# GpSimd in place of VectorE for the low part of the gate weights in a mixture-of-experts kernel

## The reference

```python
weights, idx = top 2 of 8 experts for each token, from softmax(x @ gate_w.T)
h1 = einsum('td,efd->etf', x, w1) + b1        # gate weights w1, w3: 512 x 256 for each expert
h3 = einsum('td,efd->etf', x, w3) + b3
a  = swiglu(h1 * h3)                          # g = min(h[::2], 7), l = clip(h[1::2], -7, 7)
                                              # g * sigmoid(1.702 g) * (l + 1)
y  = einsum('etf,edf->etd', a, w2) + b2
out = sum over the two experts of weight * y + shared expert(x)
```

## Time and profile before

| | |
|---|---|
| median of 3 runs | 2312.86 us (2309.55 to 2316.68) |
| the profiled execution | 2297.38 us, of which the span is 2295.6 us |
| mean granted TensorE clock | 0.96 of 2.4 GHz |
| busy over the span | PE 90%, DVE 66%, ACT 74%, POOL 28% |
| L2057, the subtraction that the change moves | 43 instructions of 2.29 us |
| L1776, the additions | 142 instructions, 2.05 us each on average |

### The profile page before, as it was taken

One profiled execution on the slowest core, in us unless ns is written; L12 is line 12 of the kernel. 1 busy time (PEld: TensorE's weight loads), 2 busy tenths in 40 slices (PEclk: granted clock), 3 DMA queues, 4 the chain that ended last, 5 costly groups with the idle time before them and its releaser, 6 DMA issues. The chain is left out here.

```text
span 2295.6 us, 38125 instructions
## 1 busy us (share of the span) xinstructions
PE 2074.2 (90%) x14085; PEld 1267.4 (55%) x14085; DVE 1521.9 (66%) x2352; ACT 1701.4 (74%) x2162; POOL 645.4 (28%) x639
## 2 busy tenths in 40 slices
PE   5995999999999999999998794799999999999970
PEld 4783333333333333333332784688888888888860
DVE  4664255555555555555555896677789988998875
ACT  4663999999999999999997672433466666666645
POOL 1111000000000000000000451677345565555637
PEclk9997999999999999999999996899999999999995
DMA  5886655555444456555410682455567676677756
GB/s 184 307 290 194 139 104 105 105 102 90 73 87 87 90 100 105 105 102 75 58 37 21 220 272 108 164 179 173 193 194 208 179 179 176 173 182 178 175 167 254
DMA packets 162651, 340.50 MB, mean 148 GB/s; under 512 B 17768, under 2 KB 91624, under 8 KB 155176
## 3 DMA queue, kind: packets, MB, share of 16 engines
q1 hardware_dynamic: 130220, 284.42, 46.5%
q0 software_dynamic: 29936, 45.90, 10.7%
q10 hardware_dynamic: 2316, 7.80, 1.0%
HBM read 194.29 MB, written 143.62 MB: 147 GB/s over the span
## 5 line engine op out<-in xcount | busy, mean ns | idle before, releaser
L1108 ACT ACTIVATE att_prob<-att_scores 128x1024 f32<-128x1024 f32 (+2 forms) x1122 | 997.7, 1031 | 58.5 <-PE att_scores L1054 54.9
L1073 PE MATMUL att_out<-att_prob,att_va 128*32 128x512 f32 (+3 forms) x5000 | 576.5, 541 | 12.9 <-DVE att_prob L1140 12.9
L1054 PE MATMUL att_scores<-att_qs,att_ks 50*128 50x512 f32 (+3 forms) x2560 | 465.5, 430 | 21.2 <-DMA att_qs<-guard 17.1
L1054 PEld LDWEIGHTS att_scores<-att_qs,att_ks 50*128 50x128 f32 x2560 | 210.9, 185 | 492.5 <-ACT att_prob L1108 417.9
L1776 POOL DMA_INDIRECT sums<-moe_y,moe_token x142 | 290.9, 2048 | 265.5 <-ACT moe_y L2034 225.2
L1918 PE MATMUL moe_ps<-moe_xt_hi,moe_w_hi 128*128 128x512 f32 (+1 forms) x880 | 339.8, 386 | 10.1 <-ACT moe_h L2007 7.1
L1918 PE MATMUL moe_ps<-moe_xt_hi,moe_w_lo 128*128 128x512 f32 (+1 forms) x880 | 333.4, 379 | 0.0
L1918 PE MATMUL moe_ps<-moe_xt_lo,moe_w_hi 128*128 128x512 f32 (+1 forms) x880 | 331.9, 377 | 0.0
L1002 POOL DMA_DIRECT2D ctx_scr<-att_cout x64 | 55.1, 860 | 983.0 <-DVE att_cout L1190 944.1
L1140 DVE SCALAR_TENSOR_TENSOR att_prob<-att_prob,att_tri 128x512 f32<-128x512 f32 x224 | 144.8, 688 | 269.0 <-ACT att_prob L1108 269.0
L1073 PEld LDWEIGHTS att_out<-att_prob,att_va 128*32 128x32 f32 x5000 | 108.3, 108 | 186.3 <-issue 105.5
(11 more groups left out here) (259 smaller groups left out, 3257.5 us busy)
## 6 DMA issues: line engine op xcount, KB each, us to landing
qk_parts<-proj_qk SPq DMA_DIRECT2D x64, 512.0 KB, 4.2
keep_first_weights<-w_experts SPq DMA_DIRECT2D x22, 1412.0 KB, 6.6
moe_wraw<-w_experts SPq DMA_DIRECT2D x21, 1412.0 KB, 6.8
att_qs<-qk_parts SPq DMA_DIRECT2D x180, 128.0 KB
att_ks<-qk_parts SPq DMA_DIRECT2D x180, 128.0 KB
rows_in<-att_zeros SPq DMA_DIRECT2D x13, 1632.0 KB, 21.6
moe_rows<-rows_in SPq DMA_DIRECT2D x22, 544.0 KB, 3.8
proj_xin<-x SPq DMA_DIRECT2D x16, 512.0 KB, 3.8
```

Source lines behind the costliest of these rows:

```text
L1054: last = nc.tensor.matmul(pss[e % SBUFS][:, h, at:at + CH - q0], ks[s][rows, half, kt * P:(kt + 1) * P], qs[s][rows, half, c * CH + q0:(c ...
L1073: last = nc.tensor.matmul(pso[k % 2][strip, q0:], va[team % 2][:, kt, strip], probs_of(u)[:, h, at:at + CH - q0], start=(kt == 0), stop=(i ...
L1108: nc.scalar.activation(probs_of(u)[:, half * 2:half * 2 + 2, start:], pss[e % SBUFS][:, :, start:], ACT.Exp, scale=HD ** -0.5)\
```

## The change

In `experts` the gate weights' low part for chunks 14 to 54 is made by a new function `gate_weights` on GpSimd. In GpSimd's list it stands after the cast of the token numbers of chunk c+2 and ahead of the additions of chunk c. For chunks 0 and 1 VectorE still makes it. The semaphore `w_lo`, which counted both low parts, is split in two, and whoever waited for it now waits for the one or for both.

```diff
+                def gate_weights(c):
+                    s = c % 2
+                    pool.wait_ge(w_hi[s], loads_to(c) * 2 - 1)
+                    nc.gpsimd.tensor_tensor(w[s][1][:, 0:W13], wraw[s][:, 0:W13], w[s][0][:, 0:W13].bitcast(F32),
+                                            ALU.subtract).then_inc(w13_lo[s], 1)
+
+                gate_weights(FIRST)
                 read_tokens(FIRST)
                 read_tokens(FIRST + 1)
+                gate_weights(FIRST + 1)
                 for c in range(FIRST, AFTER):
                     if c + 2 < AFTER:
                         read_tokens(c + 2)
+                    gate_weights(c + 2)
                     add(c)
...
-                        sp.wait_ge(w_lo[s], (loads_to(c) - 1) * 2)
+                        sp.wait_ge(w13_lo[s], loads_to(c) - 1)
+                        sp.wait_ge(w2_lo[s], loads_to(c) - 1)
...
-                    pe.wait_ge(w_lo[s], loads_to(2 * n + s) * 2 - 1)
+                    pe.wait_ge(w13_lo[s], loads_to(2 * n + s))
...
-                    pe.wait_ge(w_lo[s], loads_to(2 * n + s) * 2)
+                    pe.wait_ge(w2_lo[s], loads_to(2 * n + s))
...
                 def first_weights(n, s):
                     if not new_weights(2 * n + s):
                         return
+                    if 2 * n + s >= FIRST:
+                        return
```

More of the change, by code:

```diff
@@ L1669, in experts @@
         psY = [ph.ps(f"psY{i}", [P, 2, D]) for i in range(2)]
-        w_hi, w_lo, w_bias = (ph.sem2(n) for n in ("weights_hi", "weights_lo", "biases_copied"))
+        w_hi, w_bias = (ph.sem2(n) for n in ("weights_hi", "biases_copied"))
+        w13_lo, w2_lo = (ph.sem2(n) for n in ("gate_weights_lo", "second_weights_lo"))
         turned, x_hi, x_lo = ph.sem2("rows_turned"), ph.sem2("rows_hi"), ph.sem2("rows_lo")
@@ L1874, in _ @@
                 for d in range(2):
-                    sp.wait_ge(w_lo[d], 2 * len([c for c in loads if c % 2 == d]))
+                    sp.wait_ge(w13_lo[d], len([c for c in loads if c % 2 == d]))
+                    sp.wait_ge(w2_lo[d], len([c for c in loads if c % 2 == d]))
                     sp.wait_ge(w_bias[d], len([c for c in loads if c % 2 == d]))
@@ L2055, in first_weights @@
                         return
+                    if 2 * n + s >= FIRST:
+                        return
                     dve.wait_ge(w_hi[s], loads_to(2 * n + s) * 2 - 1)
                     V.tensor_tensor(w[s][1][:, 0:W13], wraw[s][:, 0:W13], w[s][0][:, 0:W13].bitcast(F32),
-                                    ALU.subtract).then_inc(w_lo[s], 1)
+                                    ALU.subtract).then_inc(w13_lo[s], 1)
                 def rows(n, s):
@@ L2070, in second_weights @@
                     V.tensor_tensor(w[s][1][:, W13:], wraw[s][:, W13:WM], w[s][0][:, W13:].bitcast(F32),
-                                    ALU.subtract).then_inc(w_lo[s], 1)
+                                    ALU.subtract).then_inc(w2_lo[s], 1)
                 def result(n, s):
```

## The result

The changed kernel takes 2438.5 us (2435.2 to 2440.1) where the kernel before takes 2313.6 (2309.6 to 2316.7) on the same chip: a ratio of 1.054, 95% interval 1.052 to 1.056. That is 125 us slower. The forecast was slower too, but by 77 us, and 2438.5 lies above the range of 2332 to 2422.

A forecast was written before the change was run, and what follows sets the result against it. TensorE was taken as the bound, busy 529.2 of 540 us, with VectorE close behind. Wide intervals 39, narrow groups 39 and first subtractions 3 us gave +81: 2378 profiled, 2394 as a run, forecast 2390, range 2332 to 2422.

The forecast's parts named there:

- the ring: Wide steps: additions, cast, subtraction, L2083, L2087 and weighing run serially, 16.74 us a step, 16.5 to 17.3 for most landings.
- Where the new instruction lands: GpSimd's list in a wide step: subtraction runs from 10.85 to 15.35 us, after L2159 passes, and holds L2083.
- The price of one instruction: GpSimd's subtraction of 2048 columns: 4.5 us, with 4.7 as the upper end.
- The narrow groups: Seven groups of three intervals around narrow chunks: 5.5 us more for each, 39 us in all.
- The first three subtractions: Start of the routed stretch: they meet no additions and may hold L2155; between 0 and 4 us, taken as 3.
- SyncE and the semaphores: SyncE's weight loads and the split counting: loads still land more than a step ahead, 0 us.
- What could be won: TensorE's idle time in the routed stretch, the most that relieving VectorE could give back: 10.8 us.
- lands behind L2083: Rival: L2083 and L2087 finish first, TensorE's wait for weights sets 15.35 us a step; +20 to +30 us, chance 0.22.
- The two terms: `hidden` to that step's additions 16.3 us, additions to the subtraction's end 14.3; two steps share them.
- the subtraction itself is longer: Rival: VectorE's operations interrupt GpSimd's subtraction, making it say 5.5 us; 2430 us, chance 0.1.
- The faster rival: VectorE is held only briefly at L2083 and TensorE's narrow waits vanish; 10.8 us less, 2302 as a run, chance 0.06.

The follow-up runs named there:

- The port alone: Changed kernel, but GpSimd subtracts into a spare tile nobody reads and VectorE still makes the low part; 2504.2 against 2297.3 us, ratio 1.090.
- the hold alone: Changed kernel, but GpSimd subtracts into a spare tile, nobody makes the low part, TensorE waits only for the high part; 2426.7 us, ratio 1.049.
- the order forced: Changed kernel, but GpSimd's subtraction also waits until VectorE's L2159 of the chunk before is done; 2418.6 against 2312.7 us, ratio 1.046.
- the semaphores alone: Changed kernel with only the split semaphores kept, VectorE making both low parts as before; 2296.7 against 2297.3 us, ratio 1.000.
- the versions with memsets: Changed kernel, but GpSimd fills the low part with zeros in three memsets instead of subtracting, with the same waits; 2342.7 us, ratio 1.020.
- the wait for L2083: Changed kernel, but the subtraction also waits until VectorE's L2083 in the step of the chunk before is done; 2382.4 us, ratio 1.030.
- a pause of 1 us: Changed kernel with a memset of 1024 columns ahead of each GpSimd subtraction from chunk 16 on; 2422.1 against 2297.3 us, ratio 1.0546.

## Why the prediction was wrong

The direction, the mechanism and the place were right: VectorE is held by GpSimd, the ring of additions, subtraction and VectorE becomes serial, and TensorE idles. The port alone (1.090) and the hold alone (1.049) show it. What failed is the size, in these steps.

- *"Where the new instruction lands."* This is the step that failed. The times up to that point hold: the cast comes 9.8 us after L2149 (forecast 9.7). But the forecast took the order of the recorded starts for the order of the port: L2159 starts 0.24 us before the cast, so it was to pass and to hold the cast. Instead L2159 was held. From L2083 on there are 1.4 us of work up to L2149, from L2159 on there are 3.19. With the order forced, the wide interval is 16.71 us; without, 18.17. That is 17 x 1.46 = 25 us, without which the time would have been within the range.
- *"So the ring is 16.5 to 17.3 us for nearly every landing ahead of L2083."* It came from landings with 4.5 us. In the landing that happened the subtraction starts at 9.96, takes 5.16, and 3.19 us follow: 18.3, and 18.17 were measured. The range of 2365 to 2415 doesn't follow from this ring either: 38 x (16.5 to 17.3) is 627 to 657 us in place of 525, which would give 2415 to 2445.
- *The price of one instruction.* 4.5 us forecast; 4.6 us undisturbed, 5.15 as the median, since it starts within the last addition. This went unseen because the earlier trace rows show it only in a cast: that at 1831.67 also starts within the addition that ends at 1832.26. The landing and this overlap come together: where the subtraction was made to wait, it took 4.56 us again.
- *The narrow groups.* 5.5 us each forecast, 8.3 measured, 58 us instead of 39. I had the holds there too small. The narrow L2163, which the forecast's term for the groups doesn't name, took 2.7 to 4.2 us, and L2155, which it left open, took 3.7 to 5.5 and 3.9 us in the two steps behind. The narrow step's work is half-sized, so there is less to cover a hold.
- *The first three subtractions.* 3 us forecast, 2.4 to 4.2 measured. *SyncE and the semaphores*: 0 forecast; the semaphores alone gave a ratio of 1.000, and ScalarE never waits for the weights' DMA in the routed stretch.
- *TensorE's clock* has no term in the forecast. It fell after the longer waits (0.95 on average in the routed stretch). The steps of the changed kernel are as long without it, but the narrow groups of the versions with memsets and with the wait for L2083 are longer by as much as it takes away.
- *What could be won.* At the very most 10.8 us; 8 us with no subtraction at all.
- *The rival "lands behind L2083"* didn't come about by itself. Forced, its wide interval is 15.36 us, and 15.35 was worked out. The two terms hold as well: in the step at 1857.66 the subtraction ends 14.4 us after the first addition (14.3 worked out), and the next additions start 16.0 us after `hidden` (16.3). Its total is +70 us and not +20 to +30, again by the narrow groups. The third addition takes 1.63 us where it had 3.23, as the forecast had it, so L2057 was what lengthened it. (The second held addition of the earlier trace rows ends 1.51 us after VectorE's operation and not 1.42: 1827.17 + 3.23 is 1830.40.) *The rival "the subtraction itself is longer"* is true in part, by 0.6 us and for another reason than the one given. *The faster rival* needs a lock that is given up midway; the trace has none.

**Open.** Why VectorE loses the port although its record starts first. In the changed kernel L2159 starts 0.39 us ahead of the subtraction and is held, and after a pause of 1 us L2083 starts 0.33 us ahead of it and is held as well; but L2159 there starts 0.25 us ahead of the cast and passes, as it does in the kernel before (0.22 us ahead) and not in the changed one (0.24 us ahead). GpSimd's recorded starts may be late by some tenths of a us. The runs show the fact and not the reason.

## What to carry to other kernels

Moving an operation from VectorE to GpSimd frees VectorE only for the instructions that may run beside it. Before such a move, list which of VectorE's instructions in the same stretch have two operands in SBUF or are a `tensor_scalar` on one (here L2155 and L2163), and count GpSimd's whole duration (here 4.6 to 5.2 us for 2.3 us saved) as a hold ahead of the first of them. Then add the work from there to the point that GpSimd itself waits for: that sum is the new ring, and in this kernel the place of one instruction was worth 1.5 us a step. Where two engines' starts lie within 0.4 us, work out both orders and let the range span them.

## What the runs showed of the hardware

- A GpSimd operation that reads SBUF holds VectorE's two-input instructions to its end: L2159 goes from 1.23 to 6.64 us, L2083 from 0.18 to 4.91. Whoever has the port keeps it to the end of its instruction. The Trainium skill says so ("SBUF — State Buffer", Who interferes with whom), and these rows agree.
- A VectorE `tensor_scalar` with one fp32 input in SBUF is held as well: L2155 takes up to 5.54 us beside the subtraction, and memsets hold it too (0.965 us on average instead of 0.72), while the two-input L2159 isn't held by memsets at all (1.225 us). The same section of the Trainium skill states this split between reads and writes; the forecast had left L2155 open for want of a row.
- GpSimd starts its next instructions within an indirect DMA: the cast 0.98 us and the subtraction 1.13 us after the start of an addition of 1.56 us. The subtraction is then recorded 0.55 us longer, of which 0.43 us lie beside the addition.
- TensorE's granted clock falls from 2.4 to 1.2 GHz after waits: it was lowered once between 1685 and 2210 us in the kernel before (waits 10.1 us in all) and is 0.95 on average in the changed one (88.9 us).
- The subtraction of 2048 fp32 columns takes 4.6 us on GpSimd and 2.29 us on VectorE.
